# A six-layer attention and feed-forward pipeline on one core: the attention mask moves from TensorE matmuls to a ScalarE write, with a new order of the slots

## The reference

```python
def attn_layer(x, Wqkv, qs, ksc, Wo):          # 16 heads of 64 features
    q, k, v = split(x @ Wqkv)
    q, k = l2norm(q) * qs, l2norm(k) * ksc     # then rotary tables on q and k
    out = local_attention(q, k, v)             # windows of 32 tokens
    return out @ Wo
# in local_attention: a query sees its own window and the one before, at most 32 back
sim = jnp.where(mask, -jnp.finfo(sim.dtype).max, einsum(bq, bk2) * QK_SCALE)
attn = softmax(sim); out = einsum(attn, bv2)
def ffn_layer(x, g, bln, W1, b1, W2, b2):
    xn = layernorm(x) * g + bln
    a, gate = split(xn @ W1 + b1)
    return a * gelu(gate) @ W2 + b2
for i in range(DEPTH):                         # DEPTH = 6
    x = attn_layer(shift_tokens(x), ...) + x
    x = ffn_layer(shift_tokens(x), ...) + x
```

## Time and profile before

| what | value |
|---|---|
| median of 3 runs | 3563.55 us (3558.95 to 3563.68) |
| the profiled execution: its own time | 3559.2 us |
| its span, first to last instruction | 3557.4 us |
| busy: PE, DVE, ACT, POOL | 98%, 91%, 77%, 73% |
| granted TensorE clock over the span | 0.997 |
| DMA | 48 GB/s mean |

### The profile page before, as it was taken

How to read it: one execution, slowest core, us unless ns; L and a number is a source line. 1 busy time by engine, 2 the same in 40 slices (tenths; PEclk the granted TensorE clock), 3 DMA queues, 4 the chain that set the end, 5 groups by cost and what they waited for, 6 DMA issues and landing times.

```text
span 3557.4 us, 112862 instructions
## 1 busy us (share of the span) xinstructions
PE 3480.7 (98%) x45216; PEld 2617.2 (74%) x45216; DVE 3220.0 (91%) x5488; ACT 2739.7 (77%) x4727; POOL 2580.3 (73%) x2263
## 2 busy tenths in 40 slices
PE   7998899999999999999999999999999999999998
PEld 5776577777777777777777777777777777777776
DVE  6877899999999999999999999999999999999995
ACT  4665677887887887887788788788788878878876
POOL 2433887777778777778777777877877877777772
PEclk9999999999999999999999999999999999999999
DMA  1000222122112212212212221221221221121121
GB/s 44 27 2 29 55 54 57 40 60 55 47 44 57 54 47 55 54 37 57 66 38 51 54 50 44 66 51 39 54 57 37 66 51 41 44 74 49 36 51 41
DMA packets 61573, 171.67 MB, mean 48 GB/s; under 512 B 9472, under 2 KB 21248, under 8 KB 60672
## 3 DMA queue, kind: packets, MB, share of 16 engines
q1 hardware_dynamic: 61056, 164.46, 18.1%
HBM read 21.82 MB, written 4.19 MB: 7 GB/s over the span
## 4 chain that ended last, share of the span: by engine, by line
PE 96%; issue 1%; DVE 1%; ACT 1%; POOL 1%; DVEq 0%; POOLq 0%; ACTq 0%
PE bank L1008 11%; PE bank L950 10%; PE bank L989 10%; PE bank L1024 9%; PE bank L1357 8%; PE bank L901 8%; PE bank L973 7%; PE bank L903 7%; PE bank L902 7%; PE bank L1370 4%; PE bank L967 3%; PE bank L370 2%; PE bank L350 2%; PE bank L1325 1%; PE bank L335 1%; PE bank L1340 1%
## 5 line engine op out<-in xcount | busy, mean ns | idle before, releaser
L1264 POOL TENSOR_TENSOR rotbuf<-mbuf 128x512 f32<-128x512 f32 x768 | 969.0, 1272 | 510.2 <-PE bank L950 321.6
L1278 POOL TENSOR_TENSOR rotbuf<-rotbuf,rs 128x512 f32<-128x512 f32 x768 | 787.0, 1045 | 66.0 <-DVE rs L1194 66.0
L1128 DVE TENSOR_REDUCE ss<-sq 128x8 f32<-128x512 f32 x768 | 516.7, 677 | 156.4 <-ACT sq L1050 156.2
L1288 POOL TENSOR_TENSOR probs<-probs,rden 128x768 f32<-128x768 f32 x384 | 564.6, 1470 | 120.9 <-DVE rden L1230 120.9
L1147 DVE TENSOR_TENSOR mbuf<-bank,table 128x512 f32<-128x512 f32 x768 | 528.5, 688 | 13.4
L1148 DVE TENSOR_TENSOR mbuf<-bank,table 128x512 f32<-128x512 f32 x768 | 523.2, 681 | 0.0
L1050 ACT ACTIVATE sq<-bank 128x512 f32<-128x512 f32 x768 | 458.9, 598 | 53.9 <-PE bank L903 21.9
L1008 PEld LDWEIGHTS bank<-probs_t,vbuf 96*64 96x64 f32 x12288 | 389.4, 138 | 144.4 <-issue 104.3
L1070 ACT ACTIVATE kbuf<-bank 128x512 f32<-128x512 f32 x384 | 217.9, 593 | 347.1 <-PE bank L950 347.1
L950 PE MATMUL bank<-ident,rotbuf 128*128 128x128 f32 x3072 | 451.9, 275 | 15.2 <-DVE mbuf L1148 8.6
L901 PE MATMUL bank<-weights,inputs 128*128 128x512 bf16 x1152 | 442.8, 384 | 10.5 <-DVE mbuf L1148 8.2
(11 more groups left out here) (111 smaller groups left out, 6114.6 us busy)
## 6 DMA issues: line engine op xcount, KB each, us to landing
vbuf<-v_stage SPq DMA_DIRECT2D x192, 384.0 KB, 4.5
vbuf<-v_stage SPq DMA_DIRECT2D x192, 256.0 KB, 4.0
vbuf<-v_stage SPq DMA_DIRECT2D x96, 128.0 KB, 4.5
stage<-in_wqkv SPq DMA_DIRECT2D x36, 256.0 KB, 5.3
weights<-in_wo SPq DMA_DIRECT2D x6, 512.0 KB, 6.8
weights<-in_x_t SPq DMA_DIRECT2D x1, 2048.0 KB, 7.3
out_t<-weights SPq DMA_DIRECT2D x1, 2048.0 KB, 6.3
weights<-out_t SPq DMA_DIRECT2D x1, 2048.0 KB, 10.4
```

Source lines behind the costliest of these rows:

```text
L1264: e.tensor_tensor(b.rot[:, u, :], b.m1[:, u % 2, :], b.m2[:, u % 2, :], ALU.add).then_inc(s.rotated, 1)
L1278: e.tensor_tensor(v, v, r, ALU.mult).then_inc(s.scaled, 1)
L1288: e.tensor_tensor(probs, probs, b.rden[:, p % 2, :].unsqueeze(2).broadcast_to([P, 8, BLOCK_K]), ALU.mult).then_inc(s.probs, 1)
```

## The change

A new step, `act_mask`, copies the mask from SBUF into both score banks with one ScalarE instruction. The four mask matmuls go, and the score matmuls, still with `start=False`, add to what ACT wrote. The copy waits until DVE has shifted the group before it (`shifted`), as the mask matmuls did, and PE now waits for the copy (`masked`). The fifth and sixth mask tables, which only the matmuls needed, are dropped.

The lists of all four engines are written in a new order, and with them `WORK_RING`. `DVE_REACH` changes from (-6, 2) to (-5, 2). Number and form of all other instructions of a slot stay.

```diff
 WORK_RING = (
-    ("pj", 5, 1), ("up", 0, -3), ("up", 1, -3), ("up", 2, -3), ("pj", 6, 1), ("mu", 0, -2), ("pj", 7, 1),
...
+    ("t", 4, 0), ("pj", 3, 1), ("out", 0, -2), ("pj", 4, 1), ("up", 0, -3), ("up", 1, -3), ("up", 2, -3),
+    ("pj", 5, 1), ("dn", 0, -3), ("t", 5, 0), ("mu", 0, -2), ("pj", 6, 1), ("pj", 7, 1), ("v", 0, 1),
...
 def pe_scores_of(e, s, b, at, ahead, p):
-    e.wait_ge(s.shifted, k.c[4] + p)
+    e.wait_ge(s.masked, k.c[4] + (p + 1))
     if half == 0:
         e.wait_ge(s.t_copied, k.c[8] + (4 * t + 4))
-    for blk_half, parity in ((0, 0), (1, 1), (0, 1), (1, 0)):
-        r, c = slice(64 * parity, 64 * parity + 64), slice(64 * blk_half, 64 * blk_half + 64)
-        kind = 2 if blk_half == parity else 4
-        mask = b.maskb[r, kind + t, :].unsqueeze(1).broadcast_to([64, 4, BLOCK_K])
-        e.matmul(b.scores[parity][c, 0:4 * BLOCK_K].rearrange("p (h k) -> p h k", h=4), b.identb[r, r], mask,
-                 start=True, stop=False, skip_group_check=True)
...
+def act_mask(e, s, b, at, ahead, p):
+    k = at(ahead)
+    if not k.ok:
+        return
+    e.wait_ge(s.shifted, k.c[4] + p)
+    if k.m == 0 and p == 0:
+        e.wait_ge(s.x_ready, s.first_done)
+    mask = b.maskb[:, 2 + p // 2, :].unsqueeze(1).unsqueeze(1).broadcast_to([P, 2, 4, BLOCK_K])
+    e.activation(b.score_pair.rearrange("p b (h k) -> p b h k", h=4), mask, ACT.Copy).then_inc(s.masked, 1)
...
 def act_deep_slot(e, s, b, at):
...
+    act_copy_out(e, s, b, at, -1, 0)
+    act_square(e, s, b, at, 1, 4)
+    act_ff_shift(e, s, b, at, -2)
+    act_ff_gelu(e, s, b, at, -3, 0)
+    act_ff_gelu(e, s, b, at, -3, 1)
+    act_input_of(e, s, b, at, 2)
+    act_ff_gelu(e, s, b, at, -3, 2)
+    act_square(e, s, b, at, 1, 5)
+    act_exp_of(e, s, b, at, 0, 0)
+    act_copy_pt_of(e, s, b, at, -1, 2)
+    act_copy_t(e, s, b, at, 0, 5)
+    act_square(e, s, b, at, 1, 6)
+    act_mask(e, s, b, at, 0, 1)
+    act_ff_square(e, s, b, at, -2)
+    act_square(e, s, b, at, 1, 7)
...
 def dve_deep_slot(e, s, b, at):
...
+    dve_ff_gate(e, s, b, at, -2, 1)
+    dve_ff_gate(e, s, b, at, -2, 2)
+    dve_sum_squares(e, s, b, at, 2, 5)
+    dve_rope(e, s, b, at, 2, 5)
+    dve_ff_residual(e, s, b, at, -2)
+    dve_outer(e, s, b, at, -5)
+    dve_ff_centre(e, s, b, at, -1)
+    dve_sum_of(e, s, b, at, 1, 0)
+    dve_sum_squares(e, s, b, at, 2, 6)
+    dve_rope(e, s, b, at, 2, 6)
...
```

More of the change, by code:

```diff
@@ L69 @@
 ACT_REACH = (-3, 2)
-DVE_REACH = (-6, 2)
+DVE_REACH = (-5, 2)
 POOL_REACH = (-1, 2)
@@ L723, in __init__ @@
         self.scaled = sem("scaled")
+        self.masked = sem("masked")
         self.scores = sem("scores")
@@ L788, in act_deep_credit @@
     e.sem_inc(s.seeded, FIRST_N)
+    e.sem_inc(s.masked, FIRST_N * PAIRS)
     e.sem_inc(s.exps, FIRST_N * PAIRS)
@@ L1563, in pe_deep_slot @@
 def pe_deep_slot(e, s, b, at):
-    pe_project_in(e, s, b, at, 1, 5)
[L1566 to L1571, removed]
+    pe_transpose(e, s, b, at, 0, 4)
+    pe_project_in(e, s, b, at, 1, 3)
+    pe_project_out(e, s, b, at, -2)
+    pe_project_in(e, s, b, at, 1, 4)
+    pe_ff_up(e, s, b, at, -3, 0)
+    pe_scores_of(e, s, b, at, 0, 0)
@@ L1572, in pe_deep_slot @@
+    pe_transpose_probs_of(e, s, b, at, -1, 2)
+    pe_ff_up(e, s, b, at, -3, 1)
+    pe_ff_up(e, s, b, at, -3, 2)
+    pe_project_in(e, s, b, at, 1, 5)
+    pe_values_of(e, s, b, at, -1, 1)
+    pe_ff_down(e, s, b, at, -3)
+    pe_transpose(e, s, b, at, 0, 5)
+    pe_ff_mean(e, s, b, at, -2)
     pe_project_in(e, s, b, at, 1, 6)
-    pe_ff_mean(e, s, b, at, -2)
-    pe_values_of(e, s, b, at, -1, 1)
+    pe_transpose_probs_of(e, s, b, at, -1, 3)
     pe_project_in(e, s, b, at, 1, 7)
+    pe_ff_variance(e, s, b, at, -2)
@@ L1576, in pe_deep_slot @@
     pe_scores_of(e, s, b, at, 0, 1)
-    pe_ff_variance(e, s, b, at, -2)
-    pe_transpose_probs_of(e, s, b, at, -1, 3)
+    pe_values_in(e, s, b, at, 1, 0)
+    pe_values_in(e, s, b, at, 1, 1)
+    pe_transpose_probs_of(e, s, b, at, 0, 0)
     pe_transpose(e, s, b, at, 0, 6)
-    pe_values_in(e, s, b, at, 1, 1)
     pe_transpose(e, s, b, at, 0, 7)
+    pe_project_in(e, s, b, at, 2, 0)
     pe_values_in(e, s, b, at, 1, 2)
-    pe_project_in(e, s, b, at, 2, 0)
+    pe_project_in(e, s, b, at, 2, 1)
@@ new lines, in pe_deep_slot @@
+    pe_transpose(e, s, b, at, 1, 0)
+    pe_values_of(e, s, b, at, -1, 3)
+    pe_transpose(e, s, b, at, 1, 1)
+    pe_transpose(e, s, b, at, 1, 2)
+    pe_project_in(e, s, b, at, 2, 2)
+    pe_values_of(e, s, b, at, 0, 0)
+    pe_transpose(e, s, b, at, 1, 3)
+    pe_values_in(e, s, b, at, 1, 3)
+    pe_scores_of(e, s, b, at, 0, 3)
+    pe_transpose_probs_of(e, s, b, at, 0, 1)
+    pe_ff_rstd(e, s, b, at, -2)
+def act_deep_slot(e, s, b, at):
+    act_copy_out(e, s, b, at, -1, 0)
[13 more added lines that the diff above has]
+    act_square(e, s, b, at, 1, 7)
+    act_copy_out(e, s, b, at, -1, 1)
+    act_copy_pt_of(e, s, b, at, -1, 3)
+    act_copy_v(e, s, b, at, 1, 0)
+    act_copy_v(e, s, b, at, 1, 1)
+    act_seed(e, s, b, at, 1)
+    act_copy_t(e, s, b, at, 0, 6)
+    act_copy_t(e, s, b, at, 0, 7)
+    act_square(e, s, b, at, 2, 0)
+    act_copy_v(e, s, b, at, 1, 2)
+    act_mask(e, s, b, at, 0, 2)
+    act_square(e, s, b, at, 2, 1)
+    act_copy_out(e, s, b, at, -1, 2)
+    act_exp_of(e, s, b, at, 0, 1)
+    act_copy_pt_of(e, s, b, at, 0, 0)
+    act_copy_t(e, s, b, at, 1, 0)
+    act_copy_out(e, s, b, at, -1, 3)
+    act_copy_t(e, s, b, at, 1, 1)
+    act_copy_t(e, s, b, at, 1, 2)
+    act_square(e, s, b, at, 2, 2)
+    act_mask(e, s, b, at, 0, 3)
+    act_copy_t(e, s, b, at, 1, 3)
+    act_exp_of(e, s, b, at, 0, 2)
+    act_copy_v(e, s, b, at, 1, 3)
+    act_copy_t(e, s, b, at, 1, 4)
+    act_ff_affine(e, s, b, at, -2)
+    act_square(e, s, b, at, 2, 3)
+    act_exp_of(e, s, b, at, 0, 3)
+    act_copy_pt_of(e, s, b, at, 0, 1)
+    act_mask(e, s, b, at, 1, 0)
@@ new lines, in dve_deep_slot @@
+    dve_max_of(e, s, b, at, 0, 3)
+    dve_ff_norm(e, s, b, at, -2)
+    dve_shift(e, s, b, at, 0, 3)
+    dve_sum_of(e, s, b, at, 0, 2)
+    dve_sum_squares(e, s, b, at, 2, 3)
+    dve_rope(e, s, b, at, 2, 3)
+    dve_sum_of(e, s, b, at, 0, 3)
+    dve_residual_of(e, s, b, at, -1)
+    dve_sum_squares(e, s, b, at, 2, 4)
+    dve_rope(e, s, b, at, 2, 4)
+    dve_max_of(e, s, b, at, 1, 0)
+    dve_ff_gate(e, s, b, at, -2, 0)
+    dve_shift(e, s, b, at, 1, 0)
+    dve_ff_gate(e, s, b, at, -2, 1)
@@ new lines, in dve_deep_slot @@
+    dve_ff_gate(e, s, b, at, -2, 2)
[7 more added lines that the diff above has]
+    dve_rope(e, s, b, at, 2, 6)
+def pool_deep_slot(e, s, b, at):
+    pool_input_of(e, s, b, at, 2)
+    pool_rotate(e, s, b, at, 1, 6)
+    pool_scale(e, s, b, at, 1, 0)
+    pool_rotate(e, s, b, at, 1, 7)
+    pool_scale(e, s, b, at, 1, 1)
+    pool_scale(e, s, b, at, 1, 2)
+    pool_scale(e, s, b, at, 1, 3)
+    pool_scale(e, s, b, at, 1, 4)
+    pool_rotate(e, s, b, at, 2, 0)
+    pool_normalise_of(e, s, b, at, 0, 1)
+    pool_rotate(e, s, b, at, 2, 1)
+    pool_normalise_of(e, s, b, at, 0, 2)
+    pool_rotate(e, s, b, at, 2, 2)
+    pool_rotate(e, s, b, at, 2, 3)
+    pool_next_weights(e, s, b, at(0))
+    pool_normalise_of(e, s, b, at, 0, 3)
+    pool_scale(e, s, b, at, 1, 5)
+    pool_rotate(e, s, b, at, 2, 4)
+    pool_scale(e, s, b, at, 1, 6)
+    pool_scale(e, s, b, at, 1, 7)
+    pool_rotate(e, s, b, at, 2, 5)
+    pool_normalise_of(e, s, b, at, 1, 0)
@@ L1914, in constants @@
     q, k = np.arange(BLOCK_Q)[:, None], np.arange(BLOCK_K)[None, :]
[L1915 removed]
+    masks = np.zeros((P, 4, BLOCK_K), f)
     for t in range(2):
@@ L1927, in constants @@
             masks[rows, 2 + t] = np.where(ok, 0.0, big)
-            masks[64 - 64 * half:128 - 64 * half, 4 + t] = masks[rows, 2 + t]
     half = np.arange(0, DIM_HEAD, 2, dtype=f)
```

117 lines of the change are left out of this document (8 added, 109 removed), and 5 rows, old and new, of the table WORK_RING.

## The result

| | median us | range of the runs | ratio to before, 95% interval |
|---|---|---|---|
| before | 3562.94 | 3558.95 to 3563.68 | |
| after | 3695.59 | 3693.65 to 3696.90 | 1.0374 [1.0356, 1.0392] |

The kernel became 133 us slower. The forecast was 3629, with 3575 to 3670 as its range: the sign is right and half of the loss was foreseen, but the time lies above the range. The profiled execution of after took 3696.9 us, its span is 3695.1, and the granted clock is 0.994 (0.997 before).

What follows compares the result with a forecast made beforehand. PE was taken as the bound: 32.10 us alone, plus waits of 1.39 (mean) and 0.28 (variance), gave 33.77 a slot against 33.01, 70 us more in 92 slots: 3559 + 70 = 3629 us, range 3575 to 3670.

Steps and rivals of the forecast that it cites:

- PE alone, 32.10: On PE: 33.01 us a slot less 0.72 for four mask matmul groups and 0.19 for the wait at t7.
- Mask copy 0.81: On ACT: one 128x768 mask copy into PSUM takes 0.81 us, with 0.60 and 1.02 as bounds.
- The loop through the second table load, 1.39: From up1 to the mean: 6.86 us by ACT and DVE against 5.47 on PE, so PE waits 1.39 a slot.
- The variance, 0.28: At the variance matmul: PE waits 0.28 us for ACT's feed-forward square, behind pj6's square and the group 1 mask copy.
- These have some tenths to spare: At scores1, scores2 and scores3: the mask copy follows DVE's `shifted` and is there in time, with some tenths to spare.
- refine should be short: 0.9 us less on DVE: At DVE's refine: POOL has only pj6's rotation, so the first instruction drops from 1.15 us to near 0.23.
- DVE's load, 30.8 in the sum and less by refine's 0.9: On DVE: 30.8 us of work a slot; with gaps and idle 32.6. Refine was expected 0.9 shorter.
- The ends, 0 with 10 either way: Pipeline fill and drain and the first layer keep their work: 0 us, with 10 us either way.
- PE as the bound: Rival: PE stays the bound and the kernel gets faster, 32.10 us a slot, 84 us less, 3475 us; chance 8%.
- The DVE rival: Rival: POOL blocks refine and DVE's own round takes over, about 34.1 us a slot, 3659 us; chance 13%.

Runs made afterwards that it cites:

- experiment 1: Changed kernel with ACT's square of pj5 moved ahead of the second table load; 3558.51 us, ratio 0.9992.
- experiment 8: Changed kernel with ACT's normalisation of the input moved behind gelu2, the table load and the square; 3659.81 us, ratio 1.0273.
- Experiment 2: Changed kernel with one added wait: POOL's rotation of pj6 held until DVE's refinement is through; 3697.08 us, ratio 1.0383.
- 5: experiment 1 with ACT's square for the variance of the feed-forward norm also moved ahead of the mask copy for scores1; 3555.68 us, ratio 0.9978.
- 6: The kernel of 5 with DVE's shift of pair 1 also moved ahead of the refinement; 3559.60 us, ratio 0.9987.
- 7: The kernel of 6 with masks written by PE's four matmuls again, no copies on ACT; 3569.36 us, ratio 1.0016.
- experiment 9: Kernel before in its old slot order, masks copied by ACT, and t6 ahead of PT3 on PE; 3640.03 us, ratio 1.0213.
- experiment 3: Changed kernel's new order and ring, but masks written by PE's four matmuls as before, no copies on ACT; 3716.78 us, ratio 1.0436.
- experiment 10: The kernel of 5 with DVE's softmax sum of pair 0 also moved ahead of the feed-forward norm's centring; 3535.98 us, ratio 0.9922.

## Why the prediction was half right

By the steps of the forecast:

- **PE alone, 32.10.** The size is right: 32.16 in after and 32.12 in experiment 1. Its working was not, and that the sum came out is luck. The 0.18 of the earlier trace rows is the distance of two starts, and the score products behind a mask go faster than those without (0.76 against 0.83), so four masks are 0.44 to 0.50, not 0.72. The other 0.2 lies in steps for which I had no term: up0 takes 1.07 from start to start in before (2011.73 to 2012.80) and 0.95 in after (2005.48 to 2006.43), up1 and up2 together 1.83 and 1.73. What makes them shorter is not shown; the small differences of all other steps nearly cancel.
- **Mask copy 0.81.** Measured 0.81 (384 copies, mean 0.81). Right.
- **The loop through the second table load, 1.39.** Measured 1.39 at the mean, at L1157 and with 1.43 idle on DVE before ss. Experiment 1 takes it away and gets 1.43 a slot, experiment 8 takes 0.38 of it and gets 0.38. This step is shown. The load costs what the row said: the square starts 1.29 us behind the load's start (2010.97 to 2012.26). The 1.38 more that the Trainium skill (ScalarE: Activation LUTs, What ACT_TABLE_LOAD costs) would add is not there in the trace of after either.
- **The variance, 0.28.** Measured 0.37. The mask copy and the square behind it overlap by 0.07 us, not by 0.12, and the hand-overs take the rest.
- **"These have some tenths to spare"** (scores1 to scores3), and **"refine should be short: 0.9 us less on DVE".** These steps failed, and the first of them is a term that the sum put at nothing: it has no wait at scores2 and none at t0, which measure 0.17 and 0.25. I had seen that the normalise no longer met the first instruction, but not that POOL, which waits for t6, comes to its next two-input instruction just when DVE is at the second. The lock of the earlier trace rows moved by one instruction and kept its price (1.23 in the mean, 1.15 before). The price on PE is 0.17 at scores2 and 0.25 at t0. Experiment 2 shows that the refinement is the cause.
- **DVE's load, 30.8 in the sum and less by refine's 0.9.** It is 31.2. Beside the lock that stayed, the clamp takes 0.44 us where it took 0.19, and I had not looked at it. It reads only one input from SBUF, but POOL's input step now runs beside it, and in 91 slots the clamp ends 0.05 us behind the end of that step. DVE, then POOL, in after:

```profile
2019.78 0.44 DVE L1172 TENSOR_SCALAR newton_x<-ss 128x66 f32<-128x66 f32 x1
```

```profile
2018.72 1.45 POOL L1261 TENSOR_TENSOR inputs<-x_stream,inputs 64x256 bf16<-64x256 f32 x2
```

- **The ends, 0 with 10 either way.** What is left is 9 to 10 us, at the edge: 7 ahead of the first out and behind the 93rd, the rest in the first slot and in five slots at the borders of layers, which take 34.63.
- **The last layer.** I had no term for it. `dve_outer` stands behind the second residual there, and it was not in my sum. It reads two SBUF inputs (L1497) and meets POOL's rotation of pj5, which starts 0.23 us ahead, since that too had waited for the rope. DVE's timeline in after, then POOL's, then DVE's at the same place in experiment 1, where the rope is on time:

```profile
3355.85 1.32 DVE L1497 TENSOR_TENSOR weights<-weights,x_stream 128x256 f32<-128x256 f32 x1
```

```profile
3355.62 1.27 POOL L1273 TENSOR_TENSOR rotbuf<-mbuf 128x512 f32<-128x512 f32 x1 [2.43 <-DVE mbuf L1157]
```

```profile
3332.95 0.42 DVE L1500 TENSOR_TENSOR weights<-weights,x_stream 128x256 f32<-128x256 f32 x1
```

The 0.9 us more makes PE wait at v0 (0.58 from start to start), and the slot takes 35.05, in 8 slots:

```profile
3360.60 0.39 PE L903 MATMUL bank<-weights,inputs 128*128 128x512 bf16 x1 [0.51 <-DVE ss L1449]
```

The sum of what was missed: 34.34 - 33.77 = 0.57 a slot (0.06 PE's own, 0.09 variance, 0.17 scores2, 0.25 t0), in 92 slots 52 us; last layer 8 x 0.70 = 6; ends 9. That is 67, and 3629 + 67 = 3696.

Of the rivals, PE as the bound gave 3475 us. The loop taken away, it still did not come: experiments 1, 5, 6 and 7 all stay at 32.9 to 33.0. PE then is busy for 97.6 to 99.5% of the stretch. In experiments 1, 5 and 6 it has 0.7 to 0.8 us of waits, which go from one tie to the next when one is cut. My 3475 needed all of them to be gone. The DVE rival had the right cause (refine blocked), but put 34.1 a slot as a limit of DVE's load; in truth the 1.0 us counts for 0.42 at PE, on top of the loop.

How the two parts of the change share the loss:

| | masks by PE | masks by ACT |
|---|---|---|
| old order | 3563 | 3640 (experiment 9) |
| new order | 3717 (experiment 3) | 3696 |
| new order, square ahead of the load | | 3559 (experiment 1) |
| best order found | | 3536 (experiment 10) |

## What to carry to other kernels

Where banks go round in a ring, a new order is judged by its loops: for each step ask whose instruction frees its bank, and add up what stands ahead of that instruction, a table load above all. An instruction that the table set before a load serves as well as the one behind it, as the square here, belongs ahead of the load when somebody waits for it. Once PE is nearly full, a wait that is cut comes back at the next tie; look then for an engine that stands idle just ahead of work that is wanted, fill the place with work that is not, and check which bank hangs on what is put off.
